# Segment sums of the last two graph passes as scans over a 0/1 row, with rows turned by TensorE and scaled by ScalarE

## The chip, the cores and the metric

The kernel runs on one core of a Trainium2 chip. The core has TensorE (PE in the profile; its weight loads are PEld), VectorE (DVE), ScalarE (ACT), GpSimd (POOL) and SyncE (SP), which run their own instruction streams and meet at semaphores. The metric is the device time of one launch in microseconds, as the median of the runs. A smaller number is better.

## What is computed

Four graph layers follow each other on 50000 nodes with 256 features and 25000 edges, sorted by their target node `dst`. Only the last layer matters here. Cut to its core, the reference is:

```
deg_out = segment_sum(edge_weight, src);  deg_in = segment_sum(edge_weight, dst)
norm = edge_weight * rsqrt(deg_out[src] * deg_in[dst] + EPS)
h  = relu(layernorm(x))
h6 = relu(segment_sum((h  @ W6)[src] * norm[:, None], dst) + b6)
h7 = relu(segment_sum((h6 @ W7)[src] * norm[:, None], dst) + b7)
x  = x + h7 @ Wp + bp
```

Only a node that is the target of some edge has a sum that isn't empty. The kernel does the segment sum first and the product with the weights after it, which gives the same result.

## The kernel before

The edges are laid out as 196 tiles of 128 edges; a tile has one edge in each of the 128 partitions. Everything up to about 4990 us (the three layers ahead, the node pass that writes the rows of all nodes, and the setup) is left out here. Two passes end the program, and both are a `TurnedPass`. Each goes through 49 groups of G = 4 tiles, so a group is 512 edges. The loops are unrolled in the program; each engine has a software pipeline of its own, in which a body `n` holds the step of group `n` and the steps of some earlier groups ("lags"). On each engine the order is the order written, and a wait in it holds up everything behind it.

The first of the two passes reads node rows (tensor X3), the second reads the result of the first (T7).

What a group goes through in the first pass (lines 2507 to 2618):

- POOL gathers its rows by four indirect DMAs into `got` (L2442; two slots). It waits until the relu of the group two before has been done.
- DVE takes the layernorm sums (`bn_stats`, L2560), and then 17 small operations on 128x4 numbers: mean and variance (L221 to L229), the inverse root by a bit trick and three Newton steps (L150 to L163), and the shift `nm` (L2549). They form a chain, each waiting for the one before.
- ACT makes `h = relu(scale * got + shift)`, four instructions (L2609).
- DVE makes, one body later, the selection matrices `sel` (L2460: is the target of edge q that of edge p, times the norm of p) and the row `mask` (L2462).
- PE multiplies the rows by `sel` (L2474, `acc`). The result is turned: the features lie in the partitions, the edges along the free side, and each column holds the sum within its tile of the edges of the same target.
- DVE adds what the tile before carries over, `agg = mask * (last column of agg) + acc` (L2487, eight instructions a group). In the code the small operations of a later group are taken two at a time in between, by `take(steps, each)`.
- PE multiplies `agg` by W6 and adds the bias (L2589, L2591, L2592; banks `m6`), ACT makes the relu into `put` (L2616), and SP stores `put` to T7 (L2534).

The second pass (lines 2623 to 2740) has no layernorm. POOL gathers from T7 (L2442), PE multiplies by `sel` (L2474), DVE carries on (L2487), PE multiplies by W7 (L2714, `m7`), ACT makes the relu with bias (L2738, `yt`), PE multiplies by Wp (L1208, `mm`), DVE adds `xe` (the rows of X3 that SP loads, L2666) and the bias into `xb` (L2686), adds `mm` to it into `put` (L2693), and POOL scatters `put` to the output by four indirect DMAs (L2643). So POOL has eight indirect DMAs a group there, four in the first pass.

The lags of the second pass: in body `n` POOL gathers group n and scatters group n-4; PE goes over the four tiles and takes for each the `acc` of group n-1, the `m7` of group n-2 and the `mm` of group n-3 in turn.

## Time and profile before

| | us |
|---|---|
| median of three runs | 5989.73 |
| lowest, highest run | 5988.09, 6006.96 |
| span of the profiled execution | 5993.1 |
| first pass, from its first gather to the end of its last `put` | 4992.3 to 5399.6 |
| second pass, from its first gather to the start of the last scatter | 5406.3 to 5982.6 |

The two passes take the last 1000 us of the span, one sixth. Each row of a timeline below gives the start, the duration, the engine, the line, the operation and what it writes and reads. "idle before" in square brackets is the time in which the engine did nothing before the row, with what ended it. Durations of matmuls are modelled at their end, so the distance from start to start is what counts on PE.

### The profile page before, as it was taken

To read this page: it belongs to the slowest core of one execution; us is meant where nothing else is said; L and a number is where in the kernel's file an instruction comes from. 1 tells how busy PE (TensorE), PEld (TensorE's weight loads), DVE (VectorE), ACT (ScalarE), POOL (GpSimd) and SP (SyncE) were. 2 spreads that over 40 slices of the span, in tenths; PEclk is the share of its full clock that TensorE was granted. 3 is DMA by queue.
4 is the path that set the end of the run, shared out by engine and by line. 5 is a ranking of instruction groups with operands and counts; after the bars stand their busy time and mean duration, and the time that the engine had idled before them with its cause. 6 is when DMAs were issued, how large, how long until landed. Compare 5 with 4: busy or idle time off the path is not lost. (4 is left out here: it accounts for less than half of the span.)

```text
span 5993.1 us, 77451 instructions
## 1 busy us (share of the span) xinstructions
PE 4608.6 (77%) x21160; PEld 3351.9 (56%) x21160; DVE 4603.5 (77%) x13478; ACT 2965.7 (49%) x7524; POOL 3500.3 (58%) x3009
## 2 busy tenths in 40 slices
PE   3888888888884888865777778888857674887887
PEld 3666666666663666643565545555534443665555
DVE  5888888888886888847999647777768887985554
ACT  2777777777772444432444435555545552331111
POOL 3555445454524767728888278777725433546777
PEclk9999999999996999987888889999978887998998
DMA  3666666667663444425777535555536774554444
GB/s 119 239 242 247 237 243 241 244 242 244 240 236 128 125 123 129 128 71 174 256 243 250 200 110 155 147 151 155 154 103 217 249 241 151 169 159 132 140 156 130
DMA packets 651621, 1096.83 MB, mean 183 GB/s; under 512 B 88390, under 2 KB 471814, under 8 KB 651069
## 3 DMA queue, kind: packets, MB, share of 16 engines
q1 hardware_dynamic: 525754, 837.10, 41.0%
q0 software_dynamic: 125440, 254.79, 14.7%
q8 instruction: 176, 2.88, 0.2%
q14 instruction: 251, 2.06, 0.1%
HBM read 523.88 MB, written 575.95 MB: 184 GB/s over the span
## 5 line engine op out<-in xcount | busy, mean ns | idle before, releaser
L830 PE MATMUL mm<-w,tt 128*128 128x264 f32 x3136 | 736.9, 389 | 0.8 <-ACT tt L874 0.8
L830 PEld LDWEIGHTS mm<-w,tt 128*128 128x128 f32 x3136 | 585.5, 192 | 92.5 <-ACT tt L874 1.0
L1318 POOL DMA_INDIRECT aim<-F,index x392 | 551.7, 1407 | 119.5 <-issue 119.2
L768 POOL DMA_INDIRECT xd<-in_x_dram,index x196 | 218.4, 1114 | 676.0 <-DMA XD<-xd 645.1
L1318 POOL DMA_INDIRECT got<-F,index x392 | 491.9, 1255 | 204.7 <-issue 111.2
L1476 ACT ACTIVATE rows<-acc 128x260 f32<-128x260 f32 (+1 forms) x588 | 227.4, 387 | 623.4 <-PE acc L1467 623.4
L796 POOL DMA_INDIRECT place<-PLACE,place_ix x392 | 425.2, 1085 | 119.5 <-issue 119.5
L820 PE MATMUL tp<-ident,h 128*128 128x128 f32 x1568 | 236.8, 284 | 323.9 <-ACT h L914 162.0
L1463 PE MATMUL acc<-got,sel 128*128 128x260 f32 (+1 forms) x1176 | 425.8, 449 | 74.8 <-DVE sel L1438 68.2
L2487 DVE SCALAR_TENSOR_TENSOR agg<-mask,agg,acc 128x128 f32<-128x128 f32 x784 | 251.8, 343 | 253.5 <-PE acc L2474 144.2
L830 PE MATMUL mm<-wl,tt 128*128 128x264 f32 x1568 | 419.4, 389 | 6.0 <-ACT tt L874 5.8
L820 PEld LDWEIGHTS tp<-ident,h 128*128 128x128 f32 x1568 | 167.5, 141 | 426.5 <-ACT h L885 224.3
L1208 PE MATMUL kv<-wkv,ht 128*128 128x512 f32 x784 | 384.9, 615 | 0.1
L885 ACT ACTIVATE h<-xin,nm,rt 128x256 f32<-128x256 f32 x392 | 203.3, 589 | 325.2 <-DVE nm L967 325.2
L874 ACT ACTIVATE tt<-tp 128x512 f32<-128x512 f32 x588 | 314.4, 585 | 79.3 <-PE tp L820 79.3
L1467 PE MATMUL acc<-rows,carry 128*128 128x260 f32 (+1 forms) x1008 | 345.0, 426 | 7.9 <-ACT rows L1476 1.7
L1318 POOL DMA_INDIRECT got<-HL,index x196 | 216.0, 1102 | 225.9 <-PE acc L1467 173.3
L1376 PE MATMUL turned<-ident,top 128*4 128x128 f32 (+1 forms) x588 | 124.9, 380 | 283.0 <-DVE top L1368 151.5
L1463 PEld LDWEIGHTS acc<-got,sel 128*128 128x128 f32 x1176 | 250.2, 225 | 142.4 <-DVE sel L1438 82.2
L2738 ACT ACTIVATE yt<-m,b_col 128x512 f32<-128x512 f32 x98 | 67.5, 689 | 504.4 <-PE m L2714 504.4
L830 PEld LDWEIGHTS mm<-wl,tt 128*128 128x128 f32 x1568 | 260.5, 192 | 83.2 <-issue 9.2
L2442 POOL DMA_INDIRECT got<-X,index x196 | 196.6, 1003 | 180.5 <-ACT h L2609 134.7
(348 smaller groups left out, 13645.7 us busy)
## 6 DMA issues: line engine op xcount, KB each, us to landing
F<-f1o SPq DMA_DIRECT2D x97, 528.0 KB
F<-f2o SPq DMA_DIRECT2D x97, 528.0 KB, 3.4
HL<-ho SPq DMA_DIRECT2D x97, 528.0 KB, 3.7
xin<-in_x_dram SPq DMA_DIRECT2D x97, 512.0 KB
H<-h SPq DMA_DIRECT2D x97, 512.0 KB, 3.7
X<-x3o SPq DMA_DIRECT2D x97, 512.0 KB
out_dram<-oo SPq DMA_DIRECT2D x97, 512.0 KB
drow<-DSTF SPq DMA_DIRECT2D x84, 448.0 KB
```

The source lines that it names most:

```text
L768: nc.gpsimd.indirect_dma_start(out=xd[:, n % 2, t, :], out_offset=None, in_=x, in_offset=bass.IndirectOffsetOnAxis(ap=index[:, tile, 1:2], ...
L796: nc.gpsimd.indirect_dma_start(out=place[:, t, k:k + 1], out_offset=None, in_=cells, in_offset=bass.IndirectOffsetOnAxis(ap=place_ix[:, t, ...
L820: last = nc.tensor.transpose(bank[:, 2 * r + k, :], rows_t[:, 2 * q + r, k * P:(k + 1) * P], ident[:, :])
L830: last = nc.tensor.matmul(mm[PAIR[stage, q]][:, r, 0:F2W], lhs[:, q, 2 * r + k, :], w[:, k, :], start=(k == 0), stop=(k == KB - 1))
L874: nc.scalar.activation(tt[k][:, q, :, :], tp[q][:, :, :], ACT.Copy).then_inc(s["t_h"], 1)
L885: relu = nc.scalar.activation(h1[:, r, :], xin[:, a.slot4, r, :], ACT.Relu, bias=nm[:, last_turn, r:r + 1], scale=rt[:, last_turn, r:r + 1])
L1208: last = nc.tensor.matmul(acc, lhs[:, k, :], w[:, k, :], start=(k == 0), stop=(k == KB - 1))
L1318: nc.gpsimd.indirect_dma_start(out=buf[:, n % SLOTS, t, :], out_offset=None, in_=table, in_offset=bass.IndirectOffsetOnAxis(ap=index[:, n ...
L1463: nc.tensor.matmul(acc, self.sel[:, s, t, :], self.got[:, n % SLOTS, t, 0:w], start=True, stop=False)
L1467: nc.tensor.matmul(acc, self.carry[:, s, t * P:(t + 1) * P], self.rows[:, s, t - 1, :] if t else self.crow[:, :], start=False, stop=True)\
L1476: nc.scalar.activation(self.rows[:, n % 2, t, :], self.acc[tile % 2][:, 0:self.width], ACT.Copy)\
L2487: last = nc.vector.scalar_tensor_tensor(self.agg[:, sl, k, t * P:(t + 1) * P], self.mask[:, sl, t, :], before, self.acc[sl][:, t, k, :], A ...
```

## The change

The change touches the two last passes, and a few lines of the setup.

- The setup writes to DRAM a 0/1 row, SAME: 1 where an edge has the same target as the edge before it. It costs two small DMAs more; the tile `dst_before` goes.
- `sel` and `mask` are gone, and so are the eight instructions of `carry_on`. PE turns the rows as they are (`turn_rows`, eight transposes a group into PSUM banks `turned`), and DVE makes each half of the features of a whole group in one `tensor_tensor_scan` of 512 elements: `agg[i] = same[i] * agg[i-1] + turned[i]` (`running_sums`, two instructions a group).
- The norm, which was in `sel`, is now multiplied by ACT: four `Copy` instructions with a scale a group, on `h` in the first pass (after the relu) and on `got` in the second pass (before the transposes).
- `got` has three slots in place of two.
- The inverse root stays in the small operations on DVE. They are no longer interleaved with anything.
- The bodies get new lags.

The core of the diff:

```diff
-            def select(self, dve, at):
-                for t in range(G):
-                    V.tensor_scalar(self.sel[:, sl, t, :], drow[:, t, :], dst_col[:, col], norm[:, col],
-                                    ALU.is_equal, ALU.mult)
-                V.tensor_tensor(self.mask[:, sl, :, :], drow,
...
+            def turn_rows(self, pe, n, values, slot):
+                hold(pe, self.done["agg"], (n - 1) * KB, None)
                 for k in range(KB):
+                    for t in range(G):
+                        last = nc.tensor.transpose(self.turned[n % 2][k][:, t * P:(t + 1) * P],
+                                                   values[:, slot, t, k * P:(k + 1) * P], ident[:, :])
+                    last.then_inc(self.done["turned"], 1)
+            def running_sums(self, dve, n, used, count):
+                sl = n % 2
+                hold(dve, self.ctl_in[sl], 16 * (n // 2 + 1), None)
+                hold(dve, used, count, None)
                 for k in range(KB):
+                    hold(dve, self.done["turned"], n * KB + (k + 1), None)
+                    hold(dve, self.done["agg"], (n - 1) * KB + (k + 1), None)
+                    nc.vector.tensor_tensor_scan(self.agg[:, sl, k, :], self.same[:, sl, :], self.turned[sl][k][:, :],
+                                                 self.agg[:, 1 - sl, k, G * P - 1:G * P], ALU.mult, ALU.add)\
+                        .then_inc(self.done["agg"], 1)
```

The first pass, PE and ACT:

```diff
-                        b, c = at.back(2), at.back(4)
+                        b, c = n - 1, n - 3
+                        if grouped(c):
+                            for t in range(G):
                                 bank = m6[t // 2][:, t % 2, :]
                                 if t == 0:
+                                    hold(pe, d["agg"], (c + 1) * KB, None)
                                 if t % 2 == 0:
+                                    hold(pe, d["put"], c * 2 + (t // 2 - 1), None)
...
+                        if grouped(b):
+                            hold(pe, d["h"], b + 1, None)
+                            ph.turn_rows(pe, b, h, b % 2)
...
                 def _(act):
+                        c = n - 3
+                        if grouped(n):
+                            hold(act, d["stats"], n + 1, None)
                             for r in range(G):
                                 last = nc.scalar.activation(h[:, sl, r, :], ph.got[:, n % SLOTS, r, :], ACT.Relu,
...
+                            for r in range(G):
+                                last = nc.scalar.activation(h[:, sl, r, :], h[:, sl, r, :], ACT.Copy,
+                                                            scale=norm[:, tile:tile + 1])
                             last.then_inc(d["h"], 1)
+                        if grouped(c):
+                            ph.free_put(act, c)
                             for o in range(2):
+                                hold(act, d["m6"], c * 2 + (o + 1), None)
+                                nc.scalar.activation(ph.put[:, c % 2, 2 * o:2 * o + 2, :], m6[o][:, :, :],
```

The second pass, POOL, DVE and PE:

```diff
-                        j = at.back(4)
-                        if at.alive(NG):
-                            ph.gather(pool, at, bound, d["acc"], at.n * G - G)
-                        if j.alive(NG):
-                            scatter_rows(j)
+                        if grouped(n):
+                            ph.gather(pool, n, bound, d["turned"], (n - 2) * KB)
+                        if grouped(n - 3):
+                            scatter_rows(n - 3)
...
-                        b, e = at.back(1), at.back(3)
+                        e = n - 2
+                        if grouped(n):
+                            ph.running_sums(dve, n, d["m7"], (n - 1) * KB)
...
-                        b, c, e = at.back(1), at.back(2), at.back(3)
+                        c, e = n - 1, n - 2
+                        if grouped(n):
+                            hold(pe, d["scaled"], n + 1, None)
+                            ph.turn_rows(pe, n, ph.got, n % SLOTS)
                         for t in range(G):
```

On PE in the middle of the first pass, where the sum of a tile (`acc`) and the product with W6 (`m_7` is the bank of this phase) alternated:

```order
L2474 MATMUL acc_7<-sel,h 128x128 x2
L2589 MATMUL m_7<-w,agg 128x256
L2591 MATMUL m_7<-b_parts,ones 128x256
L2592 MATMUL m_7<-w,agg 128x256
L2474 MATMUL acc_7<-sel,h 128x128 x2
L2589 MATMUL m_7<-w,agg 128x256
L2591 MATMUL m_7<-b_parts,ones 128x256
L2592 MATMUL m_7<-w,agg 128x256
```

The same place now; the rows of tile products ahead of the transposes belong to group n-3, the transposes to group n-1:

```order
L2564 MATMUL m_7<-w,agg 128x256
L2566 MATMUL m_7<-b_parts,ones 128x256
L2567 MATMUL m_7<-w,agg 128x256
L2456 MATMUL turned_7<-ident,h 128x128 x8
L2564 MATMUL m_7<-w,agg 128x256
L2566 MATMUL m_7<-b_parts,ones 128x256
L2567 MATMUL m_7<-w,agg 128x256
```

All four tile products of a group now stand together ahead of the transposes of another group; before, the first `acc` of a body stood ahead of its first product.

On PE in the middle of the second pass before (`m_8` is `m7`):

```order
L2474 MATMUL acc_8<-sel,got 128x128 x2
L2714 MATMUL m_8<-agg,w 128x512
L1208 MATMUL mm_8<-wp,yt 128x256 x2
L2474 MATMUL acc_8<-sel,got 128x128 x2
L2714 MATMUL m_8<-agg,w 128x512
L1208 MATMUL mm_8<-wp,yt 128x256 x2
```

And now, one body:

```order
L2456 MATMUL turned_8<-ident,got 128x128 x8
L2687 MATMUL m_8<-agg,w 128x512
L1210 MATMUL mm_8<-wp,yt 128x256 x2
L2687 MATMUL m_8<-agg,w 128x512
L1210 MATMUL mm_8<-wp,yt 128x256 x2
L2687 MATMUL m_8<-agg,w 128x512
L1210 MATMUL mm_8<-wp,yt 128x256 x2
L2687 MATMUL m_8<-agg,w 128x512
L1210 MATMUL mm_8<-wp,yt 128x256 x2
L2456 MATMUL turned_8<-ident,got 128x128 x8
```

The transposes of group n stand in one piece ahead of the products of groups n-1 and n-2; before, it was the sums of group n-1 among the products of n-2 and n-3.

On POOL the start of the second pass before, and now:

```order
L2635 MEMSET agg 128x2048
L2442 DMA got<-T,index 128x256 x20
L2643 DMA out_dram<-put,index 50000x256 x4
L2442 DMA got<-T,index 128x256 x4
L2643 DMA out_dram<-put,index 50000x256 x4
```

```order
L2442 DMA got<-T,index 128x256 x16
L2625 DMA out_dram<-put,index 50000x256 x4
L2442 DMA got<-T,index 128x256 x4
L2625 DMA out_dram<-put,index 50000x256 x4
```

Four groups are gathered ahead of the first scatter in place of five, and this distance stays through the pass.

## Rows read from the trace of the kernel before

**Rows 1.** The page: busy time and share of the span of each engine.

```profile
PE 4608.6 (77%) x21160; PEld 3351.9 (56%) x21160; DVE 4603.5 (77%) x13478; ACT 2965.7 (49%) x7524; POOL 3500.3 (58%) x3009
```

**Rows 2.** Windows: window, length, busy us of each engine, PEclk, DMA share, GB/s.

```profile
5112.00:5350.00 238.00, 191.16 (x1090) 151.99 (x1089) 217.16 (x1029) 93.93 (x186) 121.00 (x121) 0.98 0.54 167
5473.00:5935.00 462.00, 386.77 (x1619) 268.85 (x1618) 258.04 (x644) 55.81 (x81) 364.34 (x321) 0.92 0.46 146
```

**Rows 3.** Layernorm sums, first pass: duration ns min/median/max, first and last start.

```profile
L2560 DVE BATCH_NORM_STATS2 st<-got x196: 407/409/429, 4999.0 to 5372.6; 128x6 f32<-128x256 f32 x196
```

**Rows 4.** Groups of instructions, first pass: count | busy us, mean ns | idle before.

```profile
L2487 DVE SCALAR_TENSOR_TENSOR agg<-mask,agg,acc 128x128 f32<-128x128 f32 x392 | 133.2, 342 | 7.6 <-PE m L2592 4.8 <-PE acc L2474 0.3 <-issue 0.3
...
L2460 DVE TENSOR_SCALAR sel<-drow,dst_col,norm 128x128 f32<-128x128 f32 x196 | 54.6, 344 | 3.1
...
L2462 DVE TENSOR_TENSOR mask<-drow,dst_before 128x512 f32<-128x512 f32 x49 | 33.5, 683 | 0.0
```

**Rows 5.** Timeline of DVE, start of the first pass: small operations with nothing in between.

```profile
5004.24 1.41 DVE L2560 BATCH_NORM_STATS2 st<-got 128x6 f32<-128x256 f32 x4 [0.80 <-DMA got<-X,index]
5005.68 0.17 DVE L221 TENSOR_TENSOR mean<-st 128x4 f32<-128x4 f32 x1
...
5008.66 0.16 DVE L2549 SCALAR_TENSOR_TENSOR nm<-mean,rt 128x4 f32<-128x4 f32 x1
```

**Rows 6.** A scan of an earlier pass: duration ns min/median/max, first and last start.

```profile
L1386 DVE TENSOR_TENSOR_SCAN fwd<-pen,bwd,turned x84: 2060/2061/2069, 1890.6 to 4929.7; 4x896 f32<-4x896 f32 x56, 1x896 f32<-1x896 f32 x28
```

**Rows 7.** Timeline of ACT: a scaling of an earlier pass; relu and put.

```profile
4906.80 2.92 ACT L2390 ACTIVATE got<-got,wt 128x259 f32<-128x259 f32 x7
...
5159.08 2.07 ACT L2609 ACTIVATE h<-got,nm,rt 128x256 f32<-128x256 f32 x4 [4.51 <-DVE nm L2549]
5161.06 1.05 ACT L2616 ACTIVATE put<-m 128x512 f32<-128x512 f32 x2
```

**Rows 8.** Timeline of PE: eight transposes; the starts of two tile products.

```profile
307.01 1.04 PE L820 MATMUL tp<-ident,g 128*128 128x128 f32 x8
...
5393.94 0.59 PE L2589 MATMUL m<-w,agg 128*128 128x256 f32 x2
...
5394.91 0.59 PE L2589 MATMUL m<-w,agg 128*128 128x256 f32 x2
```

**Rows 9.** Timeline of PE: the same instructions twice after 2.62 us of idle time.

```profile
2532.85 0.68 PE L1750 MATMUL mm<-w,gt 128*128 128x264 f32 x2 [2.62 <-ACT put L1775]
...
2558.32 1.22 PE L1750 MATMUL mm<-w,gt 128*128 128x264 f32 x2 [2.62 <-ACT put L1775]
```

**Rows 10.** Timeline, second pass: an indirect DMA of POOL beside DVE's `xb`; `put`.

```profile
5569.83 1.22 DVE L2686 TENSOR_TENSOR xb<-xe,rbp 128x1024 f32<-128x1024 f32 x1
...
5569.96 1.97 POOL L2442 DMA_INDIRECT got<-T,index  x1 [0.30 <-issue]
...
5571.08 1.29 DVE L2693 TENSOR_TENSOR put<-mm,xb 128x512 f32<-128x512 f32 x2
```

**Rows 11.** Timeline, second pass: PE when rows have landed, and at full clock.

```profile
5575.69 1.22 PE L2474 MATMUL acc<-sel,got 128*128 128x128 f32 x4 [5.34 <-DMA got<-T,index]
...
5579.63 0.61 PE L2474 MATMUL acc<-sel,got 128*128 128x128 f32 x4
...
5580.07 1.02 PE L2714 MATMUL m<-agg,w 128*128 128x512 f32 x2
...
5581.80 0.61 PE L2474 MATMUL acc<-sel,got 128*128 128x128 f32 x4
```

**Rows 12.** The same pass: a group whose rows landed sooner.

```profile
5707.71 1.00 POOL L2442 DMA_INDIRECT got<-T,index  x1 [0.30 <-issue]
...
5710.60 0.71 PE L2474 MATMUL acc<-sel,got 128*128 128x128 f32 x4 [1.21 <-DMA got<-T,index]
```

**Rows 13.** Scatters: ns min/median/max, first and last; the first after the last gather.

```profile
L2643 POOL DMA_INDIRECT out_dram<-put,index x196: 974/1000/1979, 5443.0 to 5982.6; - x196
...
5951.73 1.03 POOL L2643 DMA_INDIRECT out_dram<-put,index  x1 [0.30 <-issue]
```

299 lines of the change are left out of this document (125 added, 174 removed).

## The prediction

> **What bounds the kernel now.** I read the page first: in the whole program no engine stands out [rows 1], but an average over ten phases says little on two of them, so the windows of the two passes come next [rows 2]. In the first pass DVE is busy 217.2 of 238 us (91%), the others less. A group takes 7.76 us: the layernorm sums start at 4999.0 for the first time and at 5372.6 for the last, which is the fourth of its group and so 1.0 us behind the first of it, and (5371.6 - 4999.0) / 48 = 7.76 [rows 3]. It is bound by DVE. In the second pass POOL is busy 364 of 462 us, and in front of its indirect DMAs stand 0.3 us of "issue" [rows 10, 12, 13], in which it waits for nobody: eight times 0.3 is 2.4 us a group, so POOL is full. From the first scatter of group 0 to the first of group 44 it takes (5951.73 - 5443.0) / 44 = 11.56 us a group [rows 13]. Everybody else waits for POOL there, DVE above all (258 of 462 us).
>
> **What the change takes from DVE, and why that isn't the answer.** A group of the first pass loses four `sel`, one `mask` and eight `agg` instructions; by the groups of instructions they are (54.6 + 33.5 + 133.2) / 49 = 4.5 us of busy time [rows 4]. It gains two scans of 512 elements. The trace has a scan of 896 with one input in PSUM, at 2061 ns whether it has 1 or 4 partitions [rows 6]. By the elements alone that is 2061 * 512/896 = 1.18 us, with a fixed part of 0.15 to 0.2 us set apart some 1.25 us; I take 2.5 us for the two. The small operations no longer lie between the `agg` of another group: alone, the sums take 1.44 us (5005.68 - 5004.24) and the chain from the mean to the end of `nm` 5008.82 - 5005.68 = 3.14 us [rows 5]. So DVE needs 1.44 + 3.14 + 2.5 = 7.1 us a group, 0.6 less than now. That would be a gain of 48 * 0.6 = 29 us in the first pass and none in the second, where DVE has time anyway. But both passes also get a longer chain with shorter lags, and I count those chains now.
>
> **First pass, the chain.** Write s for the moment at which DVE has made the statistics of group n. ACT does four relus, 2.07 us, then four copies with the norm. The nearest row is the scaling of an earlier pass, seven in 2.92 us [rows 7], which is 0.404 us from one to the next with 0.495 for the last: four take 1.71 us. Only then does ACT write `put` of group n-3, of which the first half takes 0.58 us (half of 1.05, and a bit). In the new order of PE the tile products of group n-2 come ahead of the transposes of group n, and their first wait is for that `put`. Four tile products take 4 * 0.97 = 3.9 us [rows 8], then the transposes, of which the first four suffice for the first scan: 0.64 us (eight take 1.04 with the time in which the last comes out [rows 8]; 0.11 each goes off). DVE then scans (2.5), takes the sums of group n+2 (1.44) and its chain (3.14). That is 2.07 + 1.71 + 0.58 + 3.9 + 0.64 + 2.5 + 1.44 + 3.14 = 16.0 us, and four or five handovers between engines of some 0.05 us to 0.1 us (relu starts 0.04 us after `nm`) make 16.3. It leads from the statistics of n to those of n+2, so a group takes at least 8.1 us: more than DVE's 7.1, more than now. DVE waits about 1 us a group, for PE.
>
> PE then does 4.8 us of work a group and is idle 3.3 us in one piece. What its clock does after that, the trace tells only by neighbours: after 2.62 us of idle time the same instruction is now at full clock (2.4 GHz, 0.68 us for two), now at half (1.2 GHz, 1.22 us) [rows 9], and after 5.34 us it was at half (1.22 us for the four instructions that take 0.61 later) [rows 11]. At half speed for the first tiles PE loses what the second pass shows: the tile after the idle time takes 5579.63 - 5575.69 = 3.94 us and the next, at full clock, 5581.80 - 5579.63 = 2.17, so 1.8 us more [rows 11]; over two groups that is 0.9 each. So 8.1 to 9.0 us, and I take 8.4. The pass has 48 such steps: 48 * (8.4 - 7.76) = 31 us more. The lags at both ends are one body shorter, and the start has no `sel` to make; I take 9 us off for that (an estimate from the bodies above: about one step of the old period of 7.8 us, and `sel` of 1.1 us). **First pass: 22 us more**, between 3 and 50.
>
> **Second pass, the chain.** The scatter of group n-3 follows the gather of group n on POOL, and it needs `put` of n-3. DVE and PE make it in their body n-1, which PE now starts with the transposes of group n-1. So the rows of group n-1 must have landed and been scaled before PE may go on with groups n-2 and n-3. Counted from the end of POOL's last gather instruction for group n-1:
>
> - landing: 5575.69 - 5571.93 = 3.76 us, or 5710.60 - 5708.71 = 1.89 us [rows 10 to 12]. Behind the start of the pass PE waited for rows 18 times, 14 times with a landing of 3.4 us or more and 4 times with one below 2, so I take 3.76;
> - scaling on ACT 1.71 (the same row as above; it doesn't exist in this pass now);
> - eight transposes 1.04 with the last result;
> - four times `m7` and `mm`: from 5580.07 to 5581.80, 1.73 each, 6.92 [rows 11];
> - the second half of `put` 0.69 (two took 1.29 on DVE, overlapping a little [rows 10]), five handovers 0.5.
>
> The sum is 14.6 us at full clock. The two scans and `xb` (2.5 + 1.22) lie beside PE's 6.92 and cost nothing. PE is idle for 4.3 us or more a group, and with the first tiles at half clock, as after its 5.34 us of idle time, 1.8 us are added: 16.4.
>
> Then POOL issues four scatters and four gathers, 8 * (1.02 + 0.30) = 10.6 us [rows 12, 13], and one of them stretches by 1.0 us beside `xb` (1.97 against 1.0) [rows 10]. With this the gather of group n+1 has ended, and two groups have passed. So a group takes (14.6 + 11.6) / 2 = 13.1 us at full clock and (16.4 + 11.6) / 2 = 14.0 at half; before, the scatter was two of POOL's blocks further behind (21 us of cover in place of 10.6), and the chain was hidden. I take 13.5, between them: 44 * (13.5 - 11.56) = 85 us. The start is some 4 us sooner (an estimate: four groups are gathered ahead in place of five, 5.3 us less, but PE is colder), and behind the last gather the chain of the last four groups is bare: gather 11.6, the chain at 15.4, a body of PE at 7 and one at 4.5 are 38 us from the first scatter of group 44 to that of 48, against 5978.7 - 5951.7 = 27 now (the last scatter starts at 5982.6, three steps of 1.3 behind 5978.7 [rows 13]): 11 more. **Second pass: 92 us more**, between 13 (landing 1.89, no half clock, no stretch: (12.8 + 10.6) / 2 = 11.7, and the 7 us of the ends) and 118 (landing 4.0, 14.1 a group).
>
> The stretch beside `xb` is a place where rows and notes differ. An indirect DMA of POOL that starts just after `xb`, a `tensor_tensor` with both inputs in SBUF, takes 1.97 us instead of 1.0 [rows 10]. The Trainium skill, page "SBUF — State Buffer", section "Who interferes with whom", infers that such an instruction doesn't hold up descriptor generation, because it takes only the read side of the shared ports; by that rule the second pass would be 0.5 us a group shorter than I have it, some 22 us in all. The row speaks against it. `mask` was of the same kind and is gone, which takes some 0.3 us a group off POOL; while POOL waits for `put` that is worth nothing.
>
> **The rest.** The two added DMAs of the setup, the dropped copy and the third slot of `got` I put at 0: the setup lies thousands of us earlier and the slot only lets POOL run ahead. The third slot does move the wait of the gathers, from the group two before to three before, and no gather waits any more.
>
> **The sum.** 5993.1 + 22 + 92 = 6107 us for a profiled execution. The median of the runs lies 3.4 us below the span of the profiled one: 6104.
>
> **The rivals.**
>
> *DVE's relief counts.* If the bodies overlap better than I counted, the first pass is bound by DVE at 7.2 us, 48 * (7.76 - 7.2) = 27 us and the 9 us of the ends less, and the second by POOL without `mask`, 44 * 0.3 = 13 less: 5993 - 49 - 3 = 5941. It decides itself at two points: the chain from the end of a gather to `put` must be under 11.5 us in the second pass (I count 14.6 to 16.4), that of the first under 14.4 (I count 16.3). For it speaks DVE's 91%; against it that the new order on PE puts products of an old group on the path of the new one, in both passes. The Trainium skill, "Perfetto Trace Analysis", section "Optimizing Scalar/DVE Operations", says that where DVE is saturated it may make sense to move work to ScalarE. By that rule this rival is what happens. Chance 0.10.
>
> *Only the first pass loses.* The second stays near POOL's pace, as landing is 1.9 us when the loads of SP fall elsewhere, and the clock holds: 11.7 to 12.5 us a group, 13 to 48 us more. With the first pass at 3 to 22, the time is 6006 to 6060. For it speaks that 4 of the 18 waits for rows were short. Chance 0.17.
>
> *The clock falls everywhere*, and landing takes 4 us and more, since scatters, gathers and loads bunch up: more than 6155. Chance 0.06.
>
> **How the numbers follow.** My forecast, both chains bare, covers 6060 to 6155 with a chance of 0.67. A range from 6005 to 6155 also takes in nearly all of the second rival and is left out by some 0.18. Against the 5989.7 of before, 0.3% is 18 us, about what a measurement can tell: faster than 5972 is the first rival alone, 0.10; between 5972 and 6008 lies the lower end of the second, 0.05; slower 0.85.
>
> **What would show it.** In the changed kernel's trace the layernorm sums should lie 8.1 to 9.0 us apart, DVE's scans should wait for the transposes, and the first tile product of a body for `put` on ACT. In the second pass POOL should wait 3 to 5 us in every second group or 2 to 2.5 us in each, for `put`, in front of a scatter; PE should wait for ACT's scaling with the granted clock below 0.9. A scan should take 1.2 to 1.3 us. I am wrong if POOL shows no wait but "issue", if a scan is much longer than 1.3 us (above 1.8 DVE binds the first pass again), or if the sums lie under 7.5 us apart.

## The result and the profile after

The changed kernel takes 6102.94 us (median of four runs, 6093.18 to 6108.36), against 5991.31 us for the kernel before in the same set. The ratio is 1.0176, with a 95% interval of 1.016 to 1.0192: it is slower, by about the amount predicted (6104). The profiled execution has a span of 6106.5 us. The agreement of the totals is partly luck, though: the first pass cost 27 us more than predicted, the second 41 us less, and 13 us lie ahead of both passes, in no step of the prediction.

That is 113.4 us more than the span before, 5993.1. The following rows are one line's instructions each, with the shortest, median and longest duration in ns and the first and last start: the layernorm sums (compare [rows 3]), the scans, the scatters (compare [rows 13]).

```profile
L2544 DVE BATCH_NORM_STATS2 st<-got x196: 400/409/428, 5012.2 to 5440.4; 128x6 f32<-128x256 f32 x196
...
L2469 DVE TENSOR_TENSOR_SCAN agg<-same,agg,turned x196: 1253/1268/1283, 5021.9 to 6069.1; 128x512 f32<-128x512 f32 x196
...
L2625 POOL DMA_INDIRECT out_dram<-put,index x196: 972/976/1899, 5500.0 to 6093.9; - x196
```

In the first pass a group now takes (5439.4 - 5012.2) / 48 = 8.90 us, where it took 7.76 (the last of the sums is the fourth of its group, 1.0 us behind the first, as in [rows 3]). In the second the first scatter of group 0 starts at 5500.03 and that of group 44 at 6051.91, which is 12.54 us a group, where it took 11.56. The ledger of the span, from the first gathers of the passes:

| | before | after | difference |
|---|---|---|---|
| start of the first pass | 4992.3 | 5005.4 | +13.1 |
| first pass, to the first gather of the second | 414.0 | 463.1 | +49.1 |
| second pass, to the end | 586.8 | 638.0 | +51.2 |
| span | 5993.1 | 6106.5 | +113.4 |

The windows of the two passes (length, busy us of PE, its weight loads, DVE, ACT and POOL with the number of instructions, granted clock as a share of 2.4 GHz, DMA share, GB/s) answer to [rows 2]:

```profile
4995.00:5440.00 445.00, 275.79 (x1276) 212.71 (x1276) 303.63 (x1107) 223.87 (x471) 197.22 (x197) 0.79 0.46 140
5530.00:6040.00 510.00, 365.55 (x1299) 242.27 (x1297) 200.91 (x204) 126.16 (x246) 341.92 (x329) 0.90 0.41 136
```

No engine is full any more: DVE is busy 68% of the first window and POOL 67% of the second. The time went into chains. The waits of the first pass (engine and line, what it waited for, us in total, times, longest):

```profile
POOL got L2442 <- ACT h L2585: 177.6, 43, 7.2
...
PE m L2564 <- ACT put L2598: 134.9, 29, 6.3
DVE agg L2469 <- PE turned L2456: 98.7, 22, 5.3
```

And of the second:

```profile
PE turned L2456 <- ACT got L2709: 161.3, 46, 6.2
POOL out_dram L2625 <- DVE put L2669: 108.1, 34, 11.0
```

One turn of the first pass's chain, which covers two groups, stands in the timeline of the changed kernel (start, duration, engine, line, operation; in brackets the idle time before it and what ended it):

```profile
5211.45 2.45 DVE L2469 TENSOR_TENSOR_SCAN agg<-same,agg,turned 128x512 f32<-128x512 f32 x2 [5.33 <-PE turned L2456]
...
5213.82 1.38 DVE L2544 BATCH_NORM_STATS2 st<-got 128x6 f32<-128x256 f32 x4
...
5218.28 2.07 ACT L2585 ACTIVATE h<-got,nm,rt 128x256 f32<-128x256 f32 x4 [6.83 <-DVE nm L2549]
...
5220.39 1.70 ACT L2591 ACTIVATE h<-h,norm 128x256 f32<-128x256 f32 x4
...
5222.00 1.05 ACT L2598 ACTIVATE put<-m 128x512 f32<-128x512 f32 x2
...
5222.71 1.19 PE L2564 MATMUL m<-w,agg 128*128 128x256 f32 x2 [6.24 <-ACT put L2598]
...
5228.70 1.03 PE L2456 MATMUL turned<-ident,h 128*128 128x128 f32 x8
...
5229.50 2.45 DVE L2469 TENSOR_TENSOR_SCAN agg<-same,agg,turned 128x512 f32<-128x512 f32 x2 [4.11 <-PE turned L2456]
```

From scan to scan: 6.83 us until relu starts (two scans, the sums, the small operations), 4.43 until PE may start (relu, scaling, the first half of `put`), 5.99 for four tile products, 0.80 until the first scan. That is 18.05 us for two groups, 9.0 for one, as the mean of the pass has it (8.90).

The second pass, two groups (SP issues the load `xe` in it; this will matter):

```profile
5683.18 0.37 SPq L2647 DMA_DIRECT2D xe<-X  x1
...
5685.69 1.00 POOL L2442 DMA_INDIRECT got<-T,index  x1 [0.30 <-issue]
...
5689.01 1.70 ACT L2709 ACTIVATE got<-got,norm 128x256 f32<-128x256 f32 x4 [2.44 <-DMA got<-T,index]
...
5690.77 1.78 PE L2456 MATMUL turned<-ident,got 128*128 128x128 f32 x8 [4.06 <-ACT got L2709]
...
5695.54 0.37 SPq L2647 DMA_DIRECT2D xe<-X  x1
...
5696.88 1.00 POOL L2442 DMA_INDIRECT got<-T,index  x1 [0.30 <-issue]
...
5700.47 0.69 DVE L2669 TENSOR_TENSOR put<-mm,xb 128x512 f32<-128x512 f32 x1 [2.65 <-PE mm L1210]
5701.01 1.70 ACT L2709 ACTIVATE got<-got,norm 128x256 f32<-128x256 f32 x4 [0.72 <-DMA got<-T,index]
5701.44 1.03 POOL L2625 DMA_INDIRECT out_dram<-put,index  x1 [3.56 <-DVE put L2669]
```

The gather ends at 5686.69, its rows have landed by 5689.01, and the scatter that needs `put` behind them starts at 5701.44: a chain of 14.75 us. POOL fills it with its own scatters and gathers, but for 1.02 us in front of the scatters before (it waited for their `put`) and the last 3.56 us.

### The profile page after: what moved, and what is told of

It reads as the page before. It is cut to its first block and busy times, and to the rows that moved or that the text cites. A ratio compares the mean times of both kernels' runs of the same rounds, so it can differ in the third digit from the quotient of the medians.

```text
span 6106.5 us, 75057 instructions
## 1 busy us (share of the span) xinstructions
PE 4575.1 (75%) x20376; PEld 3304.4 (54%) x20376; DVE 4490.6 (74%) x12398; ACT 3132.4 (51%) x7916; POOL 3461.3 (57%) x3009
## 5 line engine op out<-in xcount | busy, mean ns | idle before, releaser
L2469 DVE TENSOR_TENSOR_SCAN agg<-same,agg,turned 128x512 f32<-128x512 f32 x196 | 240.3, 1268 | 316.1 <-PE turned L2456 313.4
L2442 POOL DMA_INDIRECT got<-X,index x196 | 195.4, 997 | 224.3 <-ACT h L2585 177.6
L1128 POOL DMA_INDIRECT got<-H,index x196 | 234.0, 1194 | 95.6 <-issue 49.4
```

The lines of the kernel that those rows point to most:

```text
L1128: nc.gpsimd.indirect_dma_start(out=self.got[k][:, at.slot, t, :], out_offset=None, in_=table, in_offset=bass.IndirectOffsetOnAxis(ap=index ...
L2442: nc.gpsimd.indirect_dma_start(out=self.got[:, n % SLOTS, t, :], out_offset=None, in_=self.table, in_offset=bass.IndirectOffsetOnAxis(ap=i ...
L2469: nc.vector.tensor_tensor_scan(self.agg[:, sl, k, :], self.same[:, sl, :], self.turned[sl][k][:, :], self.agg[:, 1 - sl, k, G * P - 1:G * ...
```

## The experiments

Each set of runs has its own runs of the kernel before, which took 6059.8 us in the first set, 6061.6 in the second and 5992.9 in the third, and every ratio is to the runs of its own set. The changed kernel was 1.8% slower at first and 1.0% slower when it ran again in set 2. The us per group come from the profiled executions, worked out as above.

| | set | median us | ratio (95%) | first pass, us a group | second pass, us a group |
|---|---|---|---|---|---|
| changed kernel | – | 6102.94 | 1.0176 (1.016, 1.0192) | 8.90 | 12.54 |
| e1_turn_first_b | 1 | 6131.95 | 1.0116 (1.01, 1.0131) | 8.79 | 12.66 |
| e2_scatter_lag4_b | 1 | 6092.6 | 1.0059 (1.0043, 1.0074) | 9.01 | 11.73 |
| e3_both_b | 1 | 6085.76 | 1.0044 (1.003, 1.0057) | 8.78 | 11.86 |
| e4_pe_filled_b | 1 | 6089.07 | one run | 8.14 | 12.56 |
| c1_changed_again | 2 | 6124.39 | 1.0104 (1.0086, 1.0121) | 9.01 | 12.59 |
| e5_agg3 | 2 | 6037.14 | 0.996 (0.9949, 0.9972) | 6.96 | 12.64 |
| e6_lags_as_before | 2 | 6123.23 | 1.0105 (1.0088, 1.0122) | 9.00 | 12.54 |
| e7_all | 2 | 6043.52 | 0.9971 (0.996, 0.9981) | 7.00 | 12.71 |
| e9_before_lag3 | 3 | 6100.92 | 1.0175 (1.0158, 1.0192) | 7.74 | 13.67 |
| e8_no_norm | 3 | 6065.05 | one run | 8.34 | 12.56 |
| e10_put3_lag4 | 3 | 5920.85 | 0.988 (0.9864, 0.9897) | 6.88 | 10.93 |
| e11_put3_lag4_bias | 3 | 5904.54 | 0.9854 (0.9838, 0.9871) | 6.87 | 10.47 |

### The first pass: order, slots, clock and the scaling

**e1_turn_first_b.** PE turns group n-1 ahead of its products of group n-3.

```diff
                         b, c = n - 1, n - 3
+                        if grouped(b):
+                            hold(pe, d["h"], b + 1, None)
+                            ph.turn_rows(pe, b, h, b % 2)
                         if grouped(c):
...
-                        if grouped(b):
-                            hold(pe, d["h"], b + 1, None)
-                            ph.turn_rows(pe, b, h, b % 2)
```

> The changed kernel with one thing moved: in the first pass PE turns the rows of group n-1 ahead of the tile products of group n-3, not behind them. My theory (the order on PE puts the wait for ACT's put and four tile products into the chain between two groups' statistics): DVE binds the first pass again, its layernorm sums lie 7.1 to 7.3 us apart in place of 8.9, the pass is 75 to 85 us shorter, the whole about 6023 us; the second pass stays. Rival (the new work itself is the cost: two scans on DVE at 2.45 us and four copies more on ACT at 1.7): the same work in another order, so the sums stay 8.5 us or more apart and the time within 15 us of 6103.

A miss: 8.79 us a group, where the same pass as in the changed kernel took 9.01 in this set (e2 below). Next to nothing is gained. The rival's 8.5 or more came true, but not by its mechanism. The trace of e1 says why, first in the list of waits of its first pass:

```profile
DVE agg L2469 <- PE m L2570: 70.2, 19, 4.3
```

and in its timeline:

```profile
5206.69 2.45 DVE L2469 TENSOR_TENSOR_SCAN agg<-same,agg,turned 128x512 f32<-128x512 f32 x2 [3.85 <-PE m L2570]
```

The scan of group b writes the slot of `agg` that the products of b-2 read, and those now stand behind the transposes of b. With two slots the products are on the path by either order: I had seen the order and not the slot.

**e4_pe_filled_b.** The changed kernel, with 28 transposes a group of `ident` into a spare bank behind PE's body of the first pass, which compute nothing anybody reads.

```diff
                             ph.turn_rows(pe, b, h, b % 2)
+                            for k in range(28):
+                                nc.tensor.transpose(spare[:, 0:P], ident[:, :], ident[:, :])
```

> The changed kernel, and in the first pass 28 transposes of the identity into a spare bank on PE behind each group's eight (they are not used by anything; some 3.1 us at full clock, where PE was idle for 3.3 us a group). It tells the share of PE's half clock in the 8.9 us. If the clock is a part of it: the granted clock rises from 0.82 to over 0.95 and the sums lie 8.1 to 8.5 us apart, the pass 20 to 35 us shorter. If the chain alone makes 8.9: no change or slower, since PE has more to do.

The window of its first pass:

```profile
5115.00:5390.00 275.00, 273.35 (x1895) 237.39 (x1894) 219.85 (x782) 160.13 (x338) 134.61 (x135) 1.00 0.52 163
```

The granted clock is 1.00 (2.4 GHz) where it was 0.82 between 5115 and 5400 in the changed kernel, and a group takes 8.14 us instead of 8.90. PE did more work and the pass became shorter: the half clock behind PE's idle time is worth 0.76 us a group (0.87 against the 9.01 that this pass took in e2, in the same set; e4 ran once). The full-clock chain of the prediction, 16.3 us for two groups, is 8.15 for one.

**e8_no_norm.** The changed kernel without the four scalings by the norm in the first pass; PE's transposes wait for the relu. The norm is missing from what that pass computes.

```diff
-                            for r in range(G):
-                                tile = n * G + r
-                                last = nc.scalar.activation(h[:, sl, r, :], h[:, sl, r, :], ACT.Copy,
-                                                            scale=norm[:, tile:tile + 1])
-                            last.then_inc(d["h"], 1)
```

> The changed kernel with the four scalings by the norm left out of the first pass: PE's transposes take relu's rows directly, so the norm is missing from what is computed there. Theory (the first pass of the changed kernel is bound by one chain over two groups, relu, scaling, put half, products, transposes, scans, in which the scaling stands with 1.7 us once every two groups): 8.9 minus about 0.85 is 8.0 to 8.1 us a group. Rival (an engine is full: DVE with 7.1 us of its own work a group and its unavoidable gaps): 8.7 to 8.9, no change.

The layernorm sums of e8 (shortest, median, longest in ns; first and last start):

```profile
L2544 DVE BATCH_NORM_STATS2 st<-got x196: 398/408/428, 4996.0 to 5397.1; 128x6 f32<-128x256 f32 x196
```

and from its timeline, PE's first tile product behind the wait and the transposes behind the last:

```profile
5225.52 1.19 PE L2564 MATMUL m<-w,agg 128*128 128x256 f32 x2 [4.50 <-ACT put L2592]
...
5232.26 1.04 PE L2456 MATMUL turned<-ident,h 128*128 128x128 f32 x8
```

(5396.1 - 4996.0) / 48 = 8.34: the scaling is on the chain, since leaving it out gives 0.56 us a group. It is not the full 0.85. The timeline shows the rest. PE is idle for 4.50 us now in place of 5.7 to 6.2, and the four tile products behind that take 5232.26 - 5225.52 = 6.74 us in nearly every turn, since more of them run at half clock. In the changed kernel they take 5.50, 5.99 and 6.93 us by turns, 6.14 in the mean. That is 0.60 us over two groups, 0.30 for one, and 0.56 + 0.30 = 0.86. My number, 8.0 to 8.1, was some 0.3 us too low for that reason. e8 ran once, and its set has no run of the changed kernel.

**e5_agg3.** The order of e1, and a third slot of `agg`, in both passes.

```diff
-                self.agg = self.sb("agg", [P, 2, KB, G * P])
+                self.agg = self.sb("agg", [P, 3, KB, G * P])
...
-                            ph.running_sums(dve, b, d["m6"], (b - 1) * 2)
+                            ph.running_sums(dve, b, d["m6"], (b - 2) * 2)
```

> The changed kernel with the transposes first on PE in the first pass, and with three slots of agg in place of two. With the order alone the sums stayed 8.8 us apart, and DVE's scan waited for the tile products in place of the transposes: the scan of a group writes the slot of agg that the products of two groups before read. My theory now (the four tile products lie in the chain by two waits, the order on PE and the slots of agg; both must go): the sums 7.1 to 7.4 us apart, the pass 70 to 85 us shorter than in the changed kernel. Rival (the half clock or the copies on ACT hold the pass at 8.8): no change against the order alone.

The layernorm sums of e5:

```profile
L2544 DVE BATCH_NORM_STATS2 st<-got x196: 399/408/428, 5027.3 to 5362.6; 128x6 f32<-128x256 f32 x196
```

and the whole list of DVE's waits between 5110 and 5300:

```profile
DVE agg L2469 <- issue: 1.4, 3, 0.7
```

6.96 us a group, and 1.4 us of waiting in 190: DVE is full again, at less than it needed before, and the chain is gone. Beside c1_changed_again (below) that is 87 us less for the whole program; the first pass alone would give 48 * (9.01 - 6.96) = 98. The order alone (e1) gains 0.2 us a group and order with slot 2.05. No run has the slot alone; by the order written, the products of group b-2 would still stand ahead of the transposes of b on PE then, so it should gain nothing.

**c1_changed_again** is the changed kernel with nothing altered, to have it in the set of e5 to e7.

> The changed kernel itself, on the chip of the next three, so that they are compared with it on the same chip. Expected: 1.5 to 2% over the kernel before, the layernorm sums of the first pass 8.9 us apart, the scatters of a group in the second 12.5 us apart.

### The second pass: how far behind the scatters stand

**e2_scatter_lag4_b.** POOL scatters group n-4 behind the gather of group n, as the kernel before does; the rest as in the changed kernel.

```diff
-                        if grouped(n - 3):
-                            scatter_rows(n - 3)
+                        if grouped(n - 4):
+                            scatter_rows(n - 4)
```

> The changed kernel with one number changed: in the second pass POOL scatters group n-4 behind the gather of group n, as before the change, not n-3. My theory (in the second pass the chain from the landing of a group to the put of the group two before is longer than the two blocks of POOL's instructions that cover it): with four blocks of cover POOL doesn't wait for put any more, a step from scatter to scatter takes 11.0 to 11.5 us in place of 12.5, the pass is 45 to 65 us shorter, the whole 6040 to 6060 us. Rival (PE at half clock and ACT's scaling hold the pass back wherever the scatter stands): POOL waits elsewhere, step above 12.2, time within 15 us of 6103.

The step falls from 12.5 to 11.73 us. I had expected 11.0 to 11.5, so this is part hit and part miss. In its waits stands, for the window of the second pass:

```profile
DVE put L2669 <- DMA xe<-XD: 103.5, 30, 6.3
```

The name misleads: `xe<-XD` is a load of an earlier pass, whose semaphore this pass uses for `mm`. I took the wait to be for the slot of `put`, which the scatters of the group two before must have left, and the expectations of e6 and e10 say so. The timeline speaks against that. Here are the last scatter of the group two before, `xb`, the second of the two tile products of `mm` that the first half of `put` needs, and `put`:

```profile
5692.03 0.97 POOL L2625 DMA_INDIRECT out_dram<-put,index  x1 [0.30 <-issue]
...
5699.16 1.20 DVE L2662 TENSOR_TENSOR xb<-xe,rbp 128x1024 f32<-128x1024 f32 x1
5699.45 1.03 PE L1210 MATMUL mm<-wp,yt 128*128 128x256 f32 x4
...
5702.54 0.69 DVE L2669 TENSOR_TENSOR put<-mm,xb 128x512 f32<-128x512 f32 x1 [2.17 <-DMA xe<-XD]
```

The scatter ended 9.5 us before `put` started, and in no trace here do a group's scatters land more than 5.2 us after the end of the last of them. So the slot was free. By the rows the products had ended at 5700.48 too, and still `put` starts 2 us later. In 37 of the 98 `put` instructions of this pass DVE starts over 0.5 us after itself and the products are ready by the rows, 108 us in sum; in e3_both_b it is 33, in every other run 0 to 3. What holds `put` back in e2 and e3 isn't shown. The 11.73 us are therefore not a clean measure of what the lag is worth.

**e3_both_b** is e1 and e2 together; its first pass and its step are those of the two (8.78 and 11.86), so the two edits don't touch each other. It stays 0.4% slower than the kernel before, where I had expected it to be level or faster.

> Both moves together: transposes first on PE in the first pass, scatter one group later in the second. If the two chains are all that made the change slow, the gains add: 75 to 85 and 45 to 65 us less than 6103, so 5955 to 5985, which is level with or below the kernel before (5991). If DVE's scans or the half clock bind behind them, less: 6000 to 6060.

**e6_lags_as_before.** In the second pass the later lags of the kernel before: `mm`, `xb` and `put` of n-3, the scatter of n-4, the load of n-2. The `m7` of group n-1 stays, where the kernel before had n-2; so `m7` and `mm` of a group now lie two bodies apart, not one.

> The changed kernel with the lags of the second pass as they were: PE takes mm and DVE takes xb and put of group n-3, POOL scatters group n-4, SP loads xe of group n-2. With the scatter alone moved, a step took 11.7 us and DVE waited for a free slot of put. My theory (the chain from landing to put has twice the cover again, and a slot of put is free in time): POOL doesn't wait, a step is 11.0 to 11.4 us, the pass 50 to 65 us shorter than in the changed kernel. Rival (ACT's scaling and the transposes ahead of the products keep PE from following): 11.7 or more.

12.54 us a group, no gain: the rival's number (11.7 or more), and its mechanism. In the list of waits between 5530 and 6040:

```profile
ACT yt L2716 <- PE mm L1210: 232.8, 25, 9.8
```

`yt` has two slots, and with `mm` two bodies behind `m7`, ACT may write the `yt` of group n-1 only when PE has ended its body n. Behind that wait stands the scaling of group n+1, in order, and PE's next body starts with its transposes. So `yt`, scaling and a whole body of PE follow each other: in the timeline ACT starts `yt` at 5704.27 and again at 5716.89, 12.6 us later. e6 changes the distance from `m7` to `mm` and puts the scaling behind it in ACT's order, so it doesn't tell what the kernel before's own lags would do.

**e7_all** is e5 and e6, and the bias of the second pass as one more product on PE, so that `xb` is gone.

> Both of the others together, and the bias bp added by PE (one more matmul a tile with the bias in three bf16 parts, as for b6) in place of xb on DVE, whose two inputs in SBUF stretch POOL's indirect DMAs. If the stretch is due to xb: no indirect DMA of POOL in the second pass longer than 1.1 us, a step of 10.6 to 10.8 us. With the first pass at 7.1 to 7.4 that is 160 to 180 us less than the changed kernel and 0.8 to 1.3% less than the kernel before. If the stretch has another cause: steps of 11.1 us or more, and 0.4 to 0.8% less than before.

The first pass is that of e5 (7.00), the second that of e6 (12.71): the wait on ACT again, and taking `xb` away doesn't help a pass that waits for something else. The expected step of 10.6 to 10.8 us was missed with that. It showed one thing by itself, told in the last section.

**e9_before_lag3** asks the question from the other end: the kernel before, with nothing of the change but the lag of its scatters.

```diff
-                        j = at.back(4)
+                        j = at.back(3)
...
-                    unrolled(pool, NG, 4, group)
+                    unrolled(pool, NG, 3, group)
```

> The kernel before, with only the scatters of the second pass moved from four groups behind the gather to three, and nothing else of the change. Theory (in the second pass POOL waits for put when its three groups of own work, some 32 us, no longer cover the chain from the landing of the gather over ACT, PE and DVE to put): with a fourth group between, the kernel before is bound by POOL at 11.56 us a group; with three, the chain of landing, scaling, transposes, products and put is some 12.8 us against 10.6 us of POOL's own DMAs, so POOL is seen waiting for put and the step is 11.8 to 12.3 us, the time 15 to 40 us over the kernel before. Rival (the lag does nothing by itself, since the kernel before has no chain through scans and its put is early enough): step 11.5 to 11.7 us, within 5 us of the kernel before. The first pass should stay at 7.7 to 7.8 us a group by both, and the start of its first gather shows what of the 13 us ahead of the two passes belongs to the change.

From the timeline of its second pass:

```profile
5699.13 1.33 POOL L2442 DMA_INDIRECT got<-T,index  x1 [0.30 <-issue]
...
5703.21 1.22 PE L2474 MATMUL acc<-sel,got 128*128 128x128 f32 x4 [7.27 <-DMA got<-T,index]
...
5715.10 1.29 DVE L2693 TENSOR_TENSOR put<-mm,xb 128x512 f32<-128x512 f32 x2
...
5716.67 1.03 POOL L2643 DMA_INDIRECT out_dram<-put,index  x1 [5.76 <-DVE put L2693]
```

and from its list of waits, 5460 to 6040:

```profile
POOL out_dram L2643 <- DVE put L2693: 115.2, 21, 5.9
```

The step goes from 11.56 to 13.67 us and the whole program from 5992.9 to 6100.9. This one number costs the kernel before as much as the whole change does. Both of my numbers were too low, and the rows show the term: I had taken PE's body at full clock, 8.7 us. From the end of the gather (5700.46) it is 2.75 us until the rows are there, 11.89 until `put` starts, 1.57 until the scatter, in all 16.2; the block of four scatters and four gathers that follows ends at 5728.06, 11.4 later. (16.2 + 11.4) / 2 = 13.8. So the form of the sum by which the prediction priced the changed kernel also gives the kernel before with a lag of three, if the pieces are taken from its rows. In the kernel before these 16 us lay under 21 us of cover.

**e10_put3_lag4.** e5, with the scatters four groups behind and a third slot of `put`.

```diff
-                self.put = self.sb("put", [P, 2, G, D])
+                self.put = self.sb("put", [P, 3 if self.scatters else 2, G, D])
...
-                        if grouped(n - 3):
-                            scatter_rows(n - 3)
+                        if grouped(n - 4):
+                            scatter_rows(n - 4)
```

> The changed kernel with PE's transposes ahead of its products and three slots of agg (as e5_agg3), the scatters four groups behind the gather, and a third slot of put. Theory (with the lag back POOL's wait is gone, and the waits of DVE for a free slot of put, 95 us in e2_scatter_lag4_b, go with the third slot): first pass 7.0 us a group, second pass bound by POOL's own eight DMAs and xb, 11.0 to 11.3 us, time 0.984 to 0.990 of the kernel before. Rival (put's wait was for the landing of the scatters, which a slot only moves): second pass 11.6 to 11.8, time 0.990 to 0.993.

POOL's wait for `put` in the second pass of e10:

```profile
POOL out_dram L2625 <- DVE put L2669: 19.1, 30, 6.0
```

10.93 us a group and 0.988 of the kernel before. POOL waits 19 us in the whole pass where it waited 108. The wait of e2 on DVE is gone; DVE's `put` now waits for PE's `mm` alone. It doesn't follow that the third slot did this. In e10 each `put` starts 3.3 us or more after the scatters of the group two before have landed (2.7 and 0.9 us for the last two groups), so two slots would have been free in time as well. The third slot of `agg` makes no difference to the step at the old lag (e5, 12.64 against 12.59). What is left is the lag, four groups in place of three. No run has it alone in this set.

**e11_put3_lag4_bias.** The same, and the bias bp as a product on PE in place of DVE's `xb`.

```diff
-                            V.tensor_tensor(xb[:, :, :], xe[:, e % 2, :, :], on_tiles(rbp), ALU.add)\
-                                .then_inc(d["xb"], 1)
...
+                                nc.tensor.matmul(bank, ones3[:, :], bp_parts[:, :], start=False, stop=False)
```

> As e10_put3_lag4, and the bias bp is added by one more product on PE, so that DVE's addition xb is gone from the second pass. Theory (what is left on POOL is eight DMAs, none of them stretched beside xb): 10.6 to 10.9 us a group in the second pass, 10 to 20 us less than e10_put3_lag4, time 0.980 to 0.987 of the kernel before. Rival (a chain ahead of put is the limit in both): the same as e10_put3_lag4 within 5 us.

10.47 us a group, 0.9854 of the kernel before, the fastest here. The rows of its gathers and scatters:

```profile
L2443 POOL DMA_INDIRECT got<-T,index x196: 994/1000/1050, 5363.8 to 5855.4; - x196
...
L2626 POOL DMA_INDIRECT out_dram<-put,index x196: 971/975/1044, 5396.2 to 5888.0; - x196
```

4 * (1.000 + 0.30) + 4 * (0.975 + 0.30) = 10.3 us is what POOL's own DMAs take, and the pass is within 0.2 us of it. Of the 0.46 us between e10 and e11, 0.45 is the stretch beside `xb`: in e10 the indirect DMAs of the pass are 24.1 us longer in sum than 1.01 us each, in e11 2.4, and 21.7 / 48 = 0.45. In e11 the load `xe` waits for `put` and no longer for `xb`, so it falls elsewhere too; POOL's wait for `put` hardly changes with that (14.2 us in the pass, 19.1 in e10).

## Why the prediction was right, step by step

**The bound before.** DVE in the first pass, POOL in the second, as read from [rows 2]. e10 bears both out: with the chains off the path the first pass runs at DVE's need and the second at POOL's.

**The scan** was put at 1.25 us by elements from one of 896 [rows 6]; it takes 1.268. DVE's need of 7.1 us a group is 6.9 in e5, e10 and e11. The relief of 0.6 us was real (0.8), and it wasn't what set the time, as predicted. The Trainium skill, "Perfetto Trace Analysis", section "Optimizing Scalar/DVE Operations", says that moving work to ScalarE may make sense where DVE is saturated. In the changed kernel that lost 1.1 us a group (8.90 against 7.76), and in e5, with the same work on the same engines, it gained 0.8. The rule names the load; order and slots decided whether the load counted.

**The first pass, +22 predicted, +49 found.** The mechanism was right: the chain over relu, scaling, half of `put`, four tile products, transposes, scans, sums and small operations, with DVE waiting for PE and PE for ACT's `put`. Every piece but one was within 0.2 us. The mis-sized term is the clock of the four tile products: 5.99 us in the place of 3.9. I gave both ends, 8.1 and 9.0, and took 8.4. e4 shows that 8.1 is the full-clock end (8.14), and the pass itself sits at the other (8.90). Behind the choice stands a wrong reading of my own chain. I had PE idle for 3.3 us in every group, and it is idle for 6.24 us once in two groups, since the wait for ACT's `put` comes once in the chain and the chain covers two. The rows of 2.62 us of idle time go both ways [rows 9], but the one of 5.34 us was at half [rows 11]. With the idle time put together, the nearest row was the one at half clock, and 9.0 the end to take. The lower bound of 3 us for this pass isn't the sum's either: 48 * (8.1 - 7.76) - 9 is 7. The ends of the pass gave 54.7 - 49.1 = 5.6 us back, where I had said 9.

**The second pass, +92 predicted, +51 found.** Again the chain was the right one, and its lengths at the ends too: 38.2 us from the first scatter of group 44 to that of 48 (I said 38, it was 27 before), and 31.5 us from the first gather to the first scatter, against 36.7 (I said 4 less, it is 5). The step is what was off, 12.54 for 13.5, by three terms:

- Landing, 3.76 us predicted, has a median of 2.0 (1.73 to 4.3 in 43 groups). That is 0.9 us a group. My rows [rows 11] showed the landing of the kernel before, where the load `xe` is issued 0.84 us before the gather ends. In the changed kernel the step has other distances (last section).
- Half clock: a body of PE takes 7.6 us from its first transpose to its last product at full clock. Of the 45 bodies in the middle of the pass, 25 took 8.9 to 10.6 us; in six of these the transposes were still at full clock and the products behind them were not, and in five more than one tile was at half clock. In the mean a body is 1.0 us longer, 0.5 a group. I had 1.8 every time at the upper end, never at the lower; the middle was right here.
- The stretch of POOL's DMAs: 18.8 us in sum over the pass, 0.4 for a block of eight, where I had 1.0. Before, 87 of 392 were stretched, 42 beside `xb` and 45 beside `mask`; now 23 are, all beside `xb`.

With the measured terms the sum is (12.8 + 1.0 + 10.6 + 0.4) / 2 = 12.4, and 12.54 was found.

**The third slot of `got` and the setup at 0.** The setup holds. That no gather would wait any more doesn't: in the first pass POOL waits 177.6 us for relu, since the pass runs slower than POOL; it costs nothing.

**The 13.1 us ahead of the passes** were in no step. In the set of e8 to e11 the first gather starts at 4994.7 in the kernel before with lag 3 and at 4989.4, 4993.7 and 4998.0 in the three that carry the change. So they aren't the change's; they are a difference between executions, and the change itself is worth some 100 us of the 113. That the forecast of 6104 met 6102.94 rests on them too. In the second set the kernel before took 70 us longer (6061.6) than beside the changed kernel at first (5991.3), the changed kernel only 21 (6124.4 against 6102.9). No profile of the kernel before was taken there, and where its 70 us lay stays open, and with it whether the change costs 1.8% or 1.0%. The ratios of the first two sets are therefore smaller, and only the lengths of the stages are compared across sets.

**The rival "DVE's relief counts"** named 11.5 us as the point from which it decides in the second pass and 14.4 in the first. The chains measured 14.75 and 18.05. Its time, 5941, would have come true with the chains off the path: e10 has 5920.85, where its first pass had 7.2 and its second 11.3 us a group in my working and measured 6.88 and 10.93. In the second I had given 0.3 us a group for `mask`, and that is what it was: before, the DMAs beside `mask` were 15.0 us longer in sum, 0.3 a group. The other 0.3 comes from `xb`, beside which the stretched time fell from 36.2 us (42 DMAs above 1.2 us) to 21.7 (38) in e10.

## What to carry to other kernels

Where a pipeline's bodies are written anew, draw for each engine what stands between the end of one stage and the start of the next, and compare it with the cover that the lag gives. One lag of POOL was worth 2.1 us a group to a kernel that was otherwise not touched. An order is only as good as its slots: move a consumer ahead and look at once for who now waits for the buffer that the consumer behind it holds. When a step leaves a saturated engine, ask for the chain it joins before counting the gain.

## What the runs showed of the hardware

**A landing depends on what SP has sent last.** The time from the end of a group's last gather instruction to the first instruction that waits for its rows, against the time by which SP's issue of `xe` (128x1024 f32, 0.5 MB) lies ahead of that end, from the timelines of the second pass (groups where the engine waited for the rows; seven at the ends of the passes are left out):

| `xe` issued ahead of the gather's end by, us | kernel | groups | landing us, median (range) |
|---|---|---|---|
| 1.4 behind it | before | 4 | 1.84 (1.79 to 1.89) |
| 0.84 to 0.86 | before | 14 | 3.7 (3.4 to 5.08) |
| 0.83 to 0.85 | e10 | 29 | 3.67 (3.46 to 4.22) |
| 2.1 to 2.4 | changed | 14 | 3.26 (3.05 to 4.3) |
| 3.5 to 3.8 | changed | 7 | 2.32 (2.01 to 2.95) |
| 3.5 to 3.8 | e9 | 23 | 2.08 (1.93 to 2.88) |
| over 4.8 | changed | 22 | 1.82 (1.73 to 2.44) |
| 6.9 to 12.1 | e11 | 22 | 1.81 (1.71 to 1.91) |

From the timeline of e11, where `xe` is sent when the rows have landed (5605.24 to 5607.07 is 1.83 us):

```profile
5604.25 0.99 POOL L2443 DMA_INDIRECT got<-T,index  x1 [0.30 <-issue]
...
5607.07 1.70 ACT L2712 ACTIVATE got<-got,norm 128x256 f32<-128x256 f32 x4 [0.53 <-DMA got<-T,index]
...
5607.54 0.37 SPq L2648 DMA_DIRECT2D xe<-X  x1
```

The rows gathered come 1.8 us after the instruction when no load has been sent shortly before, and up to twice as late when one has; distance and landing sum up to 4.5 to 5.9 us in the middle rows, until the load no longer matters. The traces show what happens in between, since they count the packets of each DMA queue: q0 is POOL's queue, q1 that of SP's loads. A group of e10 whose rows are used at 5450.08, with the packets that start in the 1.5 us from 5446.5 and in the 1 us from 5448 (packets, MB, share of 16 engines):

```profile
5445.00 1.05 POOL L2442 DMA_INDIRECT got<-T,index  x1 [0.30 <-issue]
5445.20 0.37 SPq L2647 DMA_DIRECT2D xe<-X  x1
```

```profile
q1 hardware_dynamic: 337, 0.35, 77.7%
```

```profile
q1 hardware_dynamic: 230, 0.28, 76.9%
q0 software_dynamic: 43, 0.12, 30.5%
```

The last gather instruction ended at 5446.05, and between 5446.5 and 5448 no packet of POOL's queue starts. In all 29 groups of e10 in the table the 1.45 us from 0.5 us behind the gather's end hold 276 to 390 packets of SP's queue and at most 6 of POOL's; in the 22 groups of e11 a stretch of 1.3 us behind the end holds 47 to 49 of POOL's and none of SP's. So the rows come late because their packets start only when most of the load's have gone. No run moved that load alone. In the prediction it stood as half a sentence ("when the loads of SP fall elsewhere"), and as a row of its own it would have put landing right.

**POOL's indirect DMAs are stretched beside `xb` and `mask`,** the two `tensor_tensor` with both inputs in SBUF. In e7 and e11, which have neither, none of 392 is above 1.06 us; in the other kernels they go up to 2.09, and each one above 1.2 us that was counted (before, changed, e9, e10: 198) overlaps `xb` or `mask`. The Trainium skill, "SBUF — State Buffer", section "Who interferes with whom", infers that a `tensor_tensor` takes only the read side of the ports that DVE and GpSimd share, while descriptor generation needs the write side. Here the measurement decides against it: 0.45 us a group between e10 and e11. The same section also says that with both inputs in SBUF such an instruction contends with GpSimd's reads, and these DMAs read their `index` from SBUF; the trace agrees with that sentence, but no run shows which read it is. In e11 DVE's scans, with one input in PSUM, overlap 130 of these DMAs and `put` 109, and none of them is stretched.

**More work on PE, less time.** e4 adds 28 transposes a group to PE and the pass becomes 0.76 us a group shorter, since the granted clock stays at 1.00.
